# A graph layer on one core: attention denominators inverted in eight rows, and two scalings moved from VectorE to ScalarE

## The chip, the core and the metric

The kernel runs on one core of a Trainium2 chip. A core has TensorE (PE, matmuls), VectorE (DVE), ScalarE (ACT), GpSimd (POOL, which here writes the descriptors of indirect DMAs), SyncE (SP, which here issues plain DMAs), and 16 DMA engines. The metric is the device time of one execution in microseconds (us).

## What is computed

One layer over 6250 nodes of 512 features and 100000 edges sorted by target: a layer norm, a graph convolution (mean of the neighbours' rows, two products, a layer norm), linear attention in 8 heads of 64, and then a mixture of experts on the layer-normed sum. Cut to what matters:

```
xn  = layernorm(x)
q, k, v = heads(xn @ w_qkv.T);  q = elu(q / 8) + 1;  k = elu(k) + 1
denom = (q . sum_n k) per node and head + 1e-8
att = heads_joined(q @ (k^T v) / denom) @ w_out.T + b_out
mean = segment_sum(xn[src], dst) / max(deg, 1)
h   = layernorm(xn @ W_self.T + mean @ W_neigh.T + bias) * gamma + beta
x2  = x + h + att
out = x2 + shared_experts(tn) + top2_of_8_experts(tn),   tn = layernorm(x2)
```

## The kernel before

The nodes are 50 tiles of 125, taken in 25 groups of two (NG, G). There are four stages, each engine with its own written-out program and semaphores between them. First (0 to some 370 us) every row is normalised, split into two float16 halves and written to `table`; keys are made, and their sums and the context are accumulated. The weights are converted beside it. Second (to some 1750 us) comes the loop over the groups that this change touches. Third, the tokens of each expert are gathered, multiplied and written to `yd`. Fourth, the shared experts are computed and all is added up.

In the second stage the work of group i and parts of its neighbours (prev = i-1, nxt = i+1) are interleaved by hand; the order on each engine is the order in which the code is written.

- POOL (L582 to L632): for tile 0 and tile 1 of a group 17 indirect gathers of 128 rows each from `table` into a ring buffer (`gathers`, L591 and L598; ring 0 lies in the space called Wff, ring 1 in region), then four indirect scatters of token numbers into `slots` (`dispatch`, L609) for the group three before the gathered one.
- SP: edge lists (`ebuf`, L389), the transposed rows of the next group (L402), x (L408), and stores of x2 (L413) and of the normalised rows (L418, L420).
- PE (`group`, L1116): query projection (L1125), transposes of the mean (L1136), the products of tile 0 (L304 to L306), `turn_normalised` of prev (L1094), the attention denominators (L1159), `aggregate(nxt, 0)` (L1066 to L1083: 34 products of one-hot matrices with the gathered rows), gate of prev, the products of tile 1, the attention products, `places` of prev, and `aggregate(nxt, 1)`.
- DVE (`group`, L1735): minimum part of the queries (L1742), low halves, query features (L1750), the one-hot matrices of the next tile 0 (`onehots`, L1606 to L1620), the reciprocals (L1758) and products (L1761) of the attention, `means(nxt, 0)` (L1626 to L1632: degree, its reciprocal, and the division of the aggregated rows), gate of prev (L1689 to L1712), the one-hot matrices of the next tile 1, residual and first normalisation (L1774 to L1785), x2 (L1791), the second normalisation (L1380 to L1397, L1797), `means(nxt, 1)`, and `places` of prev (L1718 to L1732). `places` waits, ahead of L1727, until the scatters of `dispatch(i-2)` have landed.
- ACT: Relu and Exp of the queries, high halves (L832, L800, L845), copies out of the turned rows (L808), the denominators plus 1e-8 (L840), and the gate's Exp (L815).

The denominators: `blk_k` is a block-diagonal 128x128 matrix per 128 features with the key sums, so a product gives each of the 128 feature rows its head's denominator; ACT adds 1e-8 on the way out of PSUM, and DVE inverts all 128 rows of 500 elements twice a group.

## Time and profile before

| | |
|---|---|
| median of 3 runs | 2438.61 us (2436.04 to 2452.51) |
| profiled execution, its own time | 2446.38 us |
| its span in the trace | 2444.8 us |
| PE busy | 2094.9 us, 86% |
| DVE busy | 1728.4 us, 71% |
| POOL busy | 1476.3 us, 60% |
| ACT busy | 696.3 us, 28% |
| DMA | 497.58 MB, 204 GB/s over the span |

Busy time does not hold the time in which an engine only issues or waits. The loop of the second stage runs from about 415 us to about 1740 us of the span; its turns take a little over 50 us each. The rows below are read from that stretch: a row of a timeline is one instruction or some equal ones in a row (start, duration, engine, line, operation, output <- inputs, count, and in brackets the idle time before it and what ended it).

### The profile page before, as it was taken

To read this page: it belongs to the slowest core of one execution; us is meant where nothing else is said; L and a number is where in the kernel's file an instruction comes from. 1 tells how busy PE (TensorE), PEld (TensorE's weight loads), DVE (VectorE), ACT (ScalarE), POOL (GpSimd) and SP (SyncE) were. 2 spreads that over 40 slices of the span, in tenths; PEclk is the share of its full clock that TensorE was granted. 3 is DMA by queue.
4 is the path that set the end of the run, shared out by engine and by line. 5 is a ranking of instruction groups with operands and counts; after the bars stand their busy time and mean duration, and the time that the engine had idled before them with its cause. 6 is when DMAs were issued, how large, how long until landed. Compare 5 with 4: busy or idle time off the path is not lost.

```text
span 2444.8 us, 43895 instructions
## 1 busy us (share of the span) xinstructions
PE 2094.9 (86%) x12977; PEld 1395.4 (57%) x12978; DVE 1728.4 (71%) x3445; ACT 696.3 (28%) x1167; POOL 1476.3 (60%) x1470
## 2 busy tenths in 40 slices
PE   5988986898888788888788887888399999879999
PEld 2444543565655455555456555555266666557776
DVE  6888984888888687888688887787444444336666
ACT  3555760211122111112121111221134344323332
POOL 3665666777777777777777777774222223234442
PEclk8999998999989899999899999899599999989999
DMA  9646646777777777777877778876344454456776
GB/s 290 193 133 228 212 139 182 231 240 214 192 237 232 218 217 214 201 211 233 221 222 216 218 193 213 243 225 194 95 153 162 159 168 158 143 189 242 250 249 211
DMA packets 185852, 497.58 MB, mean 204 GB/s; under 512 B 45244, under 2 KB 58044, under 8 KB 183880
## 3 DMA queue, kind: packets, MB, share of 16 engines
q0 software_dynamic: 95984, 309.84, 44.6%
q1 hardware_dynamic: 66649, 135.52, 17.7%
q10 hardware_dynamic: 23167, 51.60, 5.4%
q8 instruction: 24, 0.39, 0.1%
q14 instruction: 28, 0.23, 0.0%
HBM read 373.97 MB, written 122.76 MB: 203 GB/s over the span
## 4 chain that ended last, share of the span: by engine, by line
PE 31%; DVE 30%; issue 14%; POOL 9%; DMA 8%; ACT 5%; DVEq 2%; SPq 1%; POOLq 0%; PEld 0%; ACTq 0%; PEldq 0%
PE bank L304 6%; DVE region L1758 6%; PE bank L305 5%; PE bank L306 5%; DMA region<-table,idx 3%; DMA slots<-tok,posi 3%; PE bank L1214 2%; DVE ohs L1606 2%; POOL Wff L598 2%; POOL region L591 2%; POOL region L540 2%; PE bank L1267 2%; PE bank L1269 2%; PE bank L1268 2%; DVE region L1405 2%
## 5 line engine op out<-in xcount | busy, mean ns | idle before, releaser
L647 POOL DMA_INDIRECT region<-table,idx x122 | 116.2, 952 | 301.0 <-PE bank L1214 264.6
L591 POOL DMA_INDIRECT region<-table,ebuf x225 | 229.1, 1018 | 79.3 <-issue 79.0
L598 POOL DMA_INDIRECT Wff<-table,ebuf x200 | 230.3, 1152 | 61.0 <-issue 61.0
L591 POOL DMA_INDIRECT Wff<-table,ebuf x225 | 221.3, 983 | 69.6 <-issue 69.6
L598 POOL DMA_INDIRECT region<-table,ebuf x200 | 223.9, 1120 | 61.0 <-issue 60.1
L304 PE MATMUL bank<-Wff,region 128*125 128x512 f16 (+1 forms) x636 | 244.8, 385 | 12.4 <-DVE region L1894 7.4
L305 PE MATMUL bank<-Wff,region 128*125 128x512 f16 (+1 forms) x636 | 244.7, 385 | 0.0
L306 PE MATMUL bank<-Wff,region 128*125 128x512 f16 (+1 forms) x636 | 244.1, 384 | 0.0
L304 PE MATMUL bank<-Wsn,region 128*125 128x512 f16 x400 | 176.0, 440 | 70.2 <-ACT region L825 67.8
L825 ACT ACTIVATE region<-bank,sv 128x500 f32<-128x500 f32 x50 | 33.7, 673 | 675.0 <-DVE region L1742 648.1
L1076 PE MATMUL bank<-region,ohs 128*125 128x512 f16 x850 | 195.7, 388 | 26.1 <-DMA region<-table,ebuf 26.1
L1758 DVE RECIPROCAL region<-region 128x500 f32<-128x500 f32 x50 | 163.7, 3273 | 41.7 <-ACT region L840 41.7
L1076 PE MATMUL bank<-Wff 128*125 128x512 f16 x850 | 189.3, 380 | 2.2 <-DMA Wff<-table,ebuf 2.2
L609 POOL DMA_INDIRECT slots<-tok,posi x100 | 129.6, 1296 | 80.4 <-DVE before L1732 50.3
L305 PE MATMUL bank<-Wsn,region 128*125 128x512 f16 x400 | 172.6, 431 | 0.0
L306 PE MATMUL bank<-Wsn,region 128*125 128x512 f16 x400 | 170.5, 426 | 0.0
L1076 PEld LDWEIGHTS bank<-region,ohs 128*125 128x125 f16 x850 | 115.6, 139 | 95.6 <-DMA region<-table,ebuf 31.0
L1859 DVE COPY region<-bank 128x1024 f16<-128x1024 f16 x60 | 41.5, 691 | 174.6 <-PE bank L1214 174.6
L1076 PEld LDWEIGHTS bank<-Wff 128*125 128x125 f16 x850 | 113.5, 137 | 67.3 <-DMA Wff<-table,ebuf 5.0
L1866 DVE SCALAR_TENSOR_TENSOR region<-bank,sv,region 128x512 f32<-128x512 f32 x118 | 88.6, 751 | 73.3 <-PE bank L306 71.2
L1225 PE MATMUL bank<-region,Wff 128*128 128x256 f16 x472 | 129.8, 275 | 1.9 <-DVE region L1859 1.9
L1226 PE MATMUL bank<-region,Wff 128*128 128x256 f16 x472 | 129.8, 275 | 0.0
(298 smaller groups left out, 5432.2 us busy)
## 6 DMA issues: line engine op xcount, KB each, us to landing
yd<-region ACTq DMA_DIRECT2D x59, 512.0 KB, 3.0
x2d<-region SPq DMA_DIRECT2D x25, 512.0 KB, 10.4
table<-region SPq DMA_DIRECT2D x25, 512.0 KB, 4.5
region<-x2d SPq DMA_DIRECT2D x25, 512.0 KB, 5.1
table<-region POOLq DMA_DIRECT2D x50, 250.0 KB, 3.4
xnt<-region POOLq DMA_DIRECT2D x25, 500.0 KB, 4.0
region<-xnt SPq DMA_DIRECT2D x25, 500.0 KB, 5.1
x2t<-region SPq DMA_DIRECT2D x25, 500.0 KB, 4.2
```

What stands on the lines that cost most here:

```text
L304: wmm(ps, xh, wh, start=first, stop=False)
L305: wmm(ps, xh, wl, start=False, stop=False)
L306: return wmm(ps, xl, wh, start=False, stop=last)
L591: pool.indirect_dma_start(out=ring[j][:, s, :], out_offset=None, in_=table, in_offset=bass.IndirectOffsetOnAxis(ap=ebuf[j][:, 2 * s:2 * s ...
L598: pool.indirect_dma_start(out=ring[j][:, s, :], out_offset=None, in_=table, in_offset=bass.IndirectOffsetOnAxis(ap=ebuf[j][:, 2 * s:2 * s ...
L609: pool.indirect_dma_start(out=slots, out_offset=bass.IndirectOffsetOnAxis(ap=posi[:, j, k:k + 1].bitcast(U32), axis=0), in_=tok[:, j:j + 1 ...
L647: pool.indirect_dma_start(out=tg[:, c, :], out_offset=None, in_=table2, in_offset=bass.IndirectOffsetOnAxis(ap=idx[:, 2 * turn + c:2 * tur ...
L1076: last = wmm(bank[6][0:T, :], oh[j][:, s, :], ring[j][:, s, part * D:(part + 1) * D], start=False, stop=False, skip_group_check=True)
L1225: wmm(ps, w1(e, 0, k, c), tTc[:, 0, k, :], start=(k == 0), stop=False)
L1226: wmm(ps, w1(e, 0, k, c), tTc[:, 1, k, :], start=False, stop=False)
L1758: dve.reciprocal(qr[:, cc, :], qr[:, cc, :]).then_inc(sem["q_rec"], 1)
L1866: stt(ysb[:, j, :], bank[4 + j][:, :], sv[:, S_W2:S_W2 + 1], b2bc[:, e, :], ALU.mult, ALU.add).then_inc(sem["y_sb"], 1)
```

## The change

Denominators: `blk_k` is replaced by `key_heads`, [128, 8] per 128 features. Four products, accumulated in one PSUM bank, give 8 rows (one per head) of 250 nodes. DVE adds 1e-8 and inverts these 8 rows in place (`den`). Then PE spreads them to the 128 feature rows of each block by four products with `head_rows` (zeros and ones, 8 x 128), behind `aggregate(nxt, 0)`; the attention product on DVE reads the spread reciprocals from PSUM. ACT's L840 is gone. In DVE's order the attention product now comes behind `means(nxt, 0)`, the gate ahead of the low halves of the queries, and the addition of beta to x ahead of `means(nxt, 0)`. ACT divides the aggregated rows by the degrees, and makes the second normalisation as x2 * rs + nm, with nm = -mean * rs from one small DVE operation. At the start some small matrices of zeros and ones are made.

```diff
-        blk_k = over[:, (OVER - 1) * FFB:(OVER - 1) * FFB + 2 * KC * 128].bitcast(F32).rearrange("p (k n) -> p k n", k=KC)
+        key_heads = tail[:, 0:KC * 8].rearrange("p (k h) -> p k h", k=KC)
+        head_rows = tail[0:8, KC * 8:KC * 8 + KC * 128]
+        den = tail[0:8, KC * 8 + KC * 128:KC * 8 + KC * 128 + GT]
...
+            def means(g, j):
+                divided = of(act, 4 * g + 2 * j + 2)
+                act.wait_ge(sem["consts"], 1)
+                act.wait_ge(sem["deg_step"], divided)
+                if past(g):
+                    act.wait_ge(sem["mt_ps"], 2 * g)
+                act.activation(mean[:, j, :], bank[6][0:T, :], ACT.Copy, scale=dg[:, j, 1:2]).then_inc(sem["mean_sb"], 1)
...
+            def normalised(i):
+                for j in range(G):
+                    act.wait_ge(sem["z_step"], (NORM_STEPS + 1) * (i + 1))
+                    if past(i):
+                        act.wait_ge(sem["tn_lo"], 2 * i)
+                    act.activation(tn[:, j, :], x2[:, j, :], ACT.Identity, scale=rs[:, j, :], bias=nm[:, j, :]).then_inc(sem["tn_sb"], 1)
...
-                for c in range(2):
-                    act.wait_ge(sem["den_ps"], 2 * i + c + 1)
-                    act.activation(qr[:, 2 * c:2 * c + 2, :], two(c), ACT.Identity, bias=tiny[:]).then_inc(sem["q_den"], 1)
+                if nxt is not None:
+                    means(nxt, 0)
...
+                if nxt is not None:
+                    means(nxt, 1)
+                normalised(i)
...
-                        for c in range(2):
-                            pe.wait_ge(sem["q_phi"], 2 * i + c + 1)
-                            for k in range(2):
-                                last = wmm(two(c)[:, k, :], blk_k[:, 2 * c + k, :], qe[:, 2 * c + k, :], start=True, stop=True)
-                            last.then_inc(sem["den_ps"], 1)
+                        for k in range(KC):
+                            pe.wait_ge(sem["q_phi"], 2 * i + k // 2 + 1)
+                            last = wmm(bank[1][0:8, 0:GT], key_heads[:, k, :], qe[:, k, :], start=(k == 0), stop=(k == KC - 1))
+                        last.then_inc(sem["den_ps"], 1)
                         if nxt is not None:
                             aggregate(nxt, 0)
+                        pe.wait_ge(sem["q_rec"], 2 * i + 2)
+                        for c in range(2):
+                            for k in range(2):
+                                last = wmm(two(c)[:, k, :], head_rows[:, (2 * c + k) * 128:(2 * c + k + 1) * 128], den, start=True, stop=True)
+                            last.then_inc(sem["spread_ps"], 1)
...
-                ts(mean[:, j, :], bank[6][0:T, :], dg[:, j, 1:2], None, ALU.mult).then_inc(sem["mean_sb"], 1)
...
             for k in range(KC):
-                ts(blk_k[:, k, :], blk[:], ksum[:, k:k + 1], None, ALU.mult).then_inc(sem["q_u"], 1)
+                ts(key_heads[:, k, :], heads[:, k, :], ksum[:, k:k + 1], None, ALU.mult).then_inc(sem["q_u"], 1)
...
+                dve.wait_ge(sem["den_ps"], i + 1)
+                if past(i):
+                    dve.wait_ge(sem["spread_ps"], 2 * i)
+                ts(den, bank[1][0:8, 0:GT], 1e-8, None, ALU.add).then_inc(sem["q_rec"], 1)
...
+                dve.reciprocal(den, den).then_inc(sem["q_rec"], 1)
+                dve.wait_ge(sem["xg_in"], 32 * (i + 1))
+                tt(xg, xg, beta_bc[0:T, None, :].broadcast_to([T, G, D]), ALU.add).then_inc(sem["h_gam"], 1)
+                if nxt is not None:
+                    means(nxt, 0)
                 for c in range(2):
-                    cc = slice(2 * c, 2 * c + 2)
-                    dve.wait_ge(sem["q_den"], 2 * i + c + 1)
-                    dve.reciprocal(qr[:, cc, :], qr[:, cc, :]).then_inc(sem["q_rec"], 1)
-                    dve.wait_ge(sem["q_rec"], 2 * i + c + 1)
-                    for k in (2 * c, 2 * c + 1):
-                        stt(qe[:, k, :], qe[:, k, :], ksum[:, k:k + 1], qr[:, k, :], ALU.mult, ALU.mult).then_inc(sem["q_hat"], 1)
+                    dve.wait_ge(sem["spread_ps"], 2 * i + c + 1)
+                    for k in range(2):
+                        stt(qe[:, 2 * c + k, :], qe[:, 2 * c + k, :], ksum[:, 2 * c + k:2 * c + k + 1], two(c)[:, k, :], ALU.mult, ALU.mult).then_inc(sem["q_hat"], 1)
+                if prev is not None:
+                    gate(prev)
...
-                for j in range(G):
-                    if past(i):
-                        dve.wait_ge(sem["tn_lo"], 2 * i)
-                    ts(tn[:, j, :], x2[:, j, :], mv[:, j, 0:1], rs[:, j, :], ALU.subtract, ALU.mult).then_inc(sem["tn_sb"], 1)
+                normal(i, x2, sem["x2_sb"], sem["z_step"], XS ** -2, 1)
+                dve.wait_ge(sem["z_step"], NORM_STEPS * (i + 1) + i)
+                stt(nm[:], mv[:, :, 0:1], -1.0, rs[:], ALU.mult, ALU.mult).then_inc(sem["z_step"], 1)
```

POOL's and SP's programs keep their order; only one semaphore that SP waits for at the end of the loop has another name.

The order on DVE, in a steady turn of the loop, from the end of the one-hot matrices of tile 0 to the gate. Before (Wff is the ring's space, `dg` the degrees, `gl` the gate's scores):

```order
L1620 TENSOR_SCALAR iota_f<-iota_f 128x125
L1758 RECIPROCAL region<-region 128x500 [waits q_den]
L1761 SCALAR_TENSOR_TENSOR region<-region,ksum 128x250 [waits q_rec]
L1761 SCALAR_TENSOR_TENSOR region<-region,ksum 128x250
L1758 RECIPROCAL region<-region 128x500 [waits q_den]
L1761 SCALAR_TENSOR_TENSOR region<-region,ksum 128x250 [waits q_rec]
L1761 SCALAR_TENSOR_TENSOR region<-region,ksum 128x250
L1765 TENSOR_TENSOR region<-region 128x500 [waits q_hi] x2
L1625 REGISTER_ALU
L1626 TENSOR_SCALAR dg<-bank 125x1 [waits agg_end]
```

And now (here Wff holds the eight rows `den`, in a part of the same space):

```order
L1657 TENSOR_SCALAR iota_f<-iota_f 128x125
L1794 TENSOR_SCALAR Wff<-bank 8x250 [waits spread_ps,den_ps]
L1798 RECIPROCAL Wff<-Wff 8x250 [waits q_rec,consts]
L1799 REGISTER_ALU
L1800 TENSOR_TENSOR region<-region,beta_bc 125x1024 [waits xg_in]
L1662 REGISTER_ALU
L1663 TENSOR_SCALAR dg<-bank 125x1 [waits agg_end]
L1664 REGISTER_ALU
L1665 RECIPROCAL dg<-dg 125x1 [waits deg_step]
L1806 SCALAR_TENSOR_TENSOR region<-region,ksum,bank 128x250 [waits spread_ps]
L1806 SCALAR_TENSOR_TENSOR region<-region,ksum,bank 128x250
```

The wait for the end of the aggregation (agg_end) now stands ahead of the attention products; it stood behind them.

On ACT, the end of one steady turn and the start of the next (L801 is the division by the degrees, L813 the second normalisation, L846 the Relu of the next group's queries), as it is now:

```order
L865 ACTIVATE region<-region 128x500 [waits att_ps,q_hat]
L832 ISA
L834 ISA [waits gate_dve]
L836 ACTIVATE ge,gs<-gl,gs 125x8 [waits gate_dve]
L837 ACTIVATE ew<-g,gs 125x2
L836 ACTIVATE ge,gs<-gl,gs 125x8
L837 ACTIVATE ew<-g,gs 125x2
L319 REGISTER_ALU
L801 ACTIVATE region<-bank,dg 125x512 [waits mt_ps,deg_step,consts]
L810 REGISTER_ALU
L813 ACTIVATE region<-region,nm,rs 125x512 [waits tn_lo,z_step] x2
```

The work of the last two ACTIVATE lines was DVE's before (L1632 and L1797); on ACT the next group's Relu followed the gate's Exp directly.

## Rows read from the trace of the kernel before

**Rows 1.** Page, part 4: the chain that ended last, by line

```profile
PE bank L304 6%; DVE region L1758 6%; PE bank L305 5%; PE bank L306 5%; DMA region<-table,idx 3%; DMA slots<-tok,posi 3%; PE bank L1214 2%; DVE ohs L1606 2%; POOL Wff L598 2%; POOL region L591 2%; POOL region L540 2%; PE bank L1267 2%; PE bank L1269 2%; PE bank L1268 2%; DVE region L1405 2%
```

**Rows 2.** Busy us (instructions) per stretch: PE, PEld, DVE, ACT, POOL; clock, DMA share, GB/s

```profile
414.90:1667.00 1252.10, 1078.08 (x6103) 719.53 (x6104) 997.31 (x2281) 231.64 (x470) 974.46 (x900) 0.93 0.78 220
561.60:1620.70 1059.10, 906.06 (x5143) 604.59 (x5142) 846.54 (x1963) 196.13 (x400) 823.85 (x761) 0.93 0.78 218
```

**Rows 3.** POOL's timeline: gathers (start us, duration us), idle before in brackets

```profile
389.57 0.95 POOL L591 DMA_INDIRECT region<-table,ebuf  x1 [7.56 <-issue]
...
956.21 0.95 POOL L591 DMA_INDIRECT region<-table,ebuf  x1 [2.95 <-issue]
...
1004.70 2.86 POOL L598 DMA_INDIRECT Wff<-table,ebuf  x1 [0.31 <-issue]
...
1065.67 0.95 POOL L591 DMA_INDIRECT region<-table,ebuf  x1 [0.30 <-issue]
```

**Rows 4.** DVE's timeline: one turn of the loop, from L1742 to L1742

```profile
1048.98 1.38 DVE L1742 TENSOR_SCALAR region<-bank,sv 128x500 f32<-128x500 f32 x2 [0.42 <-issue]
...
1065.79 0.87 DVE L1761 SCALAR_TENSOR_TENSOR region<-region,ksum 128x250 f32<-128x250 f32 x2
...
1073.08 0.23 DVE L1689 SCALAR_TENSOR_TENSOR gl<-bank,sv,gateb_bc 125x16 f32<-125x16 f32 x1
...
1077.59 2.38 DVE L1606 TENSOR_TENSOR ohs<-iota_f,ebuf 128x2125 f16<-128x2125 f32 x1 [1.71 <-issue]
...
1083.53 1.39 DVE L1777 SCALAR_TENSOR_TENSOR region<-bank,sv,bias_bc 125x512 f32<-125x512 f32 x2
...
1096.56 1.00 DVE L1797 TENSOR_SCALAR region<-region,mv,rs 125x512 f32<-125x512 f32 x2
...
1100.47 1.38 DVE L1742 TENSOR_SCALAR region<-bank,sv 128x500 f32<-128x500 f32 x2 [0.43 <-issue]
```

**Rows 5.** DVE's timeline: the wait of `places` for the scatters, once in seven turns

```profile
1211.56 0.17 DVE L1727 CAST posi<-posf 125x4 int32<-125x4 f32 x1 [10.15 <-DMA slots<-tok,posi]
```

**Rows 6.** PE's timeline in the same turn: denominators, then the aggregation of tile 0

```profile
1060.61 1.96 PE L1159 MATMUL bank<-region,Wff 128*128 128x250 f32 x8 [1.55 <-ACT region L808]
...
1063.32 7.53 PE L1076 MATMUL bank<-Wff 128*125 128x512 f16 x34
```

**Rows 7.** DVE, 561.6 to 1620.7 (20 turns): busy us, mean ns | idle before

```profile
L1758 DVE RECIPROCAL region<-region 128x500 f32<-128x500 f32 x40 | 130.9, 3274 | 30.8 <-ACT region L840 30.8
...
L1606 DVE TENSOR_TENSOR ohs<-iota_f,ebuf 128x2125 f16<-128x2125 f32 x20 | 47.5, 2375 | 33.6 <-issue 33.6
L1606 DVE TENSOR_TENSOR Wff<-iota_f,ebuf 128x2125 f16<-128x2125 f32 x20 | 47.5, 2375 | 4.5 <-issue 4.5
...
L1761 DVE SCALAR_TENSOR_TENSOR region<-region,ksum 128x250 f32<-128x250 f32 x80 | 34.8, 477 | 1.4
L1632 DVE TENSOR_SCALAR region<-bank,dg 125x512 f32<-125x512 f32 x40 | 30.0, 751 | 1.8 <-DVE dg L1628 0.5
...
L1765 DVE TENSOR_TENSOR region<-region 128x500 f16<-128x500 f32 x40 | 27.1, 677 | 1.9
...
L1774 DVE TENSOR_TENSOR region<-region,beta_bc 125x1024 f32<-125x1024 f32 x20 | 24.5, 1227 | 0.0
L1797 DVE TENSOR_SCALAR region<-region,mv,rs 125x512 f32<-125x512 f32 x40 | 20.8, 562 | 0.7
...
L1628 DVE RECIPROCAL dg<-dg 125x1 f32<-125x1 f32 x40 | 6.6, 164 | 1.8 <-DVE dg L1626 0.5
```

**Rows 8.** Page, part 5: an ACT operation out of PSUM

```profile
L825 ACT ACTIVATE region<-bank,sv 128x500 f32<-128x500 f32 x50 | 33.7, 673 | 675.0 <-DVE region L1742 648.1
```

**Rows 9.** DVE's timeline in the last group, which has no gathers behind it

```profile
1697.18 3.28 DVE L1758 RECIPROCAL region<-region 128x500 f32<-128x500 f32 x1 [6.97 <-ACT region L840]
...
1710.48 1.40 DVE L1777 SCALAR_TENSOR_TENSOR region<-bank,sv,bias_bc 125x512 f32<-125x512 f32 x2
```

**Rows 10.** POOL's timeline: the first scatter after the last group's places of prev

```profile
1726.17 1.64 POOL L609 DMA_INDIRECT slots<-tok,posi  x1 [31.10 <-DVE before L1732]
```

More of the change, by code:

```diff
@@ L816, in gate, with group @@
                     act.activation(ew[:, j, :], g8[:, j, 0:2], ACT.Exp, bias=gs[:, j, 0:1]).then_inc(sem["gate_exp"], 1)
-            def group(i, prev):
+            def group(i, prev, nxt):
                 for c in range(2):
@@ L1181, in _ @@
             pe.wait_ge(sem["ksum_sb"], 1)
-            pe.wait_ge(sem["q_u"], KC)
+            for k in range(KC):
+                last = pe.transpose(bank[1][0:8, k * 128:(k + 1) * 128], heads[:, k, :], ident[:, :])
+            last.then_inc(sem["heads_ps"], 1)
             aggregate(0, 0)
+            pe.wait_ge(sem["q_u"], 3 * KC + 2)
             turn_largest("mf_max", 1, 1, MH, 1)
```

60 lines of the change are left out of this document (34 added, 26 removed).

## The prediction

> **What bounds the kernel now.** I began with the page's chain that ended last, because it seems to speak for the change: DVE's L1758, the reciprocals of the denominators, holds 6% of the span by itself [rows 1], some 147 us, and the change makes them small. But a chain is followed back from the last instruction through whichever wait ended last, and where two loops run at nearly one pace it may pass through either. So I asked next which engine never waits in the loop.
>
> That is POOL. From the first gather of the loop's steady part to the last it executes 900 instructions in 1252.10 us and is busy for 974.46 us [rows 2]; what is left, 277.6 us, is 0.308 us per instruction. The gap between two gathers that wait for nothing is 0.30 us [rows 3]. At 0.30 us the gaps come to 270 us, so in all of the loop POOL has waited for others for at most 8 us, and one wait alone, ahead of the gather at 956.21, is 2.7 us of it [rows 3]. The larger wait, 7.56 us at 389.57, lies ahead of the loop's steady part and hangs on the context's products. A POOL that does not wait sets the pace. Its pace is 20 turns in 1059.10 us, with 761 = 20 x 38 + 1 instructions (34 gathers and 4 scatters a turn) [rows 2]: 52.96 us a turn.
>
> The other engines' turn is shorter when nothing holds them: DVE's goes from 1048.98 to 1100.47, 51.49 us [rows 4]. They catch up with POOL by 1.5 us a turn, until once in some seven turns DVE stands 10.15 us in `places` for scatters to land [rows 5]. Then they are behind again. That saw tooth costs POOL nearly nothing, and its mean is POOL's turn. In short: from 415 to 1667 us of the span the kernel is bound by POOL's writing of descriptors, and only in the last group, when there is nothing left to gather, is the chain through DVE and PE the bound.
>
> **The change part by part.** POOL's program is unchanged: the same 34 gathers and 4 scatters. So the first term is what the loop's turn becomes if POOL did not exist; it matters only if it rises above 52.96 us.
>
> Ahead of A, the end of the aggregation of tile 0, nothing gets longer. PE makes four products of 250 columns for the denominators as before, 1.96 us [rows 6], and starts the aggregation behind them; it ends with 1063.32 + 7.53 = 1070.85 [rows 6], so A is about 21.9 us after DVE's L1742. What DVE does meanwhile is hidden: the addition on eight rows, the reciprocal, and the addition of beta, 1.23 us [rows 7]. A reciprocal of 8 rows of 250 is not in this trace. Its time goes by the length of a row: 3.27 us for 500 and 0.16 us for 1 [rows 7] give 0.16 + 249 x 6.23 ns = 1.7 us (bounds: 0.16 and 3.27). Even at 3.27 us, begun after the denominators at 1062.6, it and the two additions end by 1068, ahead of A.
>
> After A things stand in a row that stood side by side. The four spreading products have the same number of columns as L1159, so 1.96 us; bounds are 0 (they overlap) and 3.9 us (at half the clock). DVE's four attention products follow each half: 4 x 0.477 = 1.9 us [rows 7], reading one input from PSUM, as L1777 does at no higher price (0.70 us for 512 elements, two overlapping rows in 1.39 us [rows 4]). The second pair ends at about A + 3.0. The gate's scores come 1.96 us later from PE than before, when DVE started on them at A + 2.2 (1073.08 [rows 4]); so at A + 4.1 at the latest. The gate itself lasts until 1077.59 - 1.71 = 1075.88, 2.8 us [rows 4], then the low halves, 2 x 0.68 us [rows 7]: A + 8.3. Before the one-hot matrices of tile 1 DVE idled 33.6 / 20 = 1.7 us a turn, before those of tile 0 4.5 / 20 = 0.2 us [rows 7]; the latter follow plain work that covers the loading of registers, as the low halves now do. So they start between A + 8.5 and A + 10.0, where they started at A + 6.7 before: 1.8 to 3.3 us later. Behind them DVE saves the addition of beta, 1.2 us, the normalisation's 1.00 us [rows 4] less about 0.2 us for the new small operation, and the division by the degrees, 0.75 us [rows 7]: 2.75 us. The division and the normalisation are now ACT's, each about the 0.67 us of a row of 500 out of PSUM [rows 8]: bounds 0.56 us (DVE's own L1797) and 0.75 us (L1632) [rows 7]. ACT makes the division first, no later than DVE did, and has finished the normalisation 1.3 us later, while DVE is in `places` and L1742; its Relu is not late. If that cover is gone, the Relu and all behind it on PE wait up to 1.3 us. The other divisions (tile 0) stand on ACT ahead of the high halves, which need the attention products made after A anyway.
>
> Turn without POOL: 51.49 + (1.8 to 3.3) - 2.75 = 50.5 to 52.0 us. DVE's busy time falls by about 2 x 3.27 + 2 x 0.75 + 1.00 - 2.3 = 6.7 us a turn, but its wait for the aggregation takes most of it. Both ends are below 52.96. The loop keeps POOL's turn, and the saving in it is 0, at most the 8 us that POOL waited.
>
> The second term is the last group, where no aggregation stands between. DVE went from its first reciprocal at 1697.18 to L1777 at 1710.48, 13.3 us [rows 9]. Now, from the same start: addition to the eight rows, 0.4, reciprocal 1.7, spread 2.0, the last pair of attention products 0.9, then the gate. Its scores wait for PE until the spread and the gate's own products are through (A + 2.2 above, so 2.0 + 1.5 after the reciprocal, with 2.8 us of gate behind them), then low halves 1.4: 0.4 + 1.7 + 3.5 + 2.8 + 1.4 = 9.8 us; the addition of beta lies under the spread. L1777 starts 3.5 us earlier, of which I keep 3, since it will also wait for PE's second tile. `places` of prev then starts another 0.8 us earlier (0.2 in place of the 1.00 us of L1797), and POOL's scatters at 1726.17, on which the expert stage hangs, wait for it [rows 10]. Together 3.8 us; bounds 0 and 4.3.
>
> The third is the phase in which the other engines leave the loop: up to 1.5 us earlier than now, or up to the 10 us of a fresh wait [rows 5] later. I take +1. Ahead of the loop small matrices of zeros and ones are made and a 128-wide product becomes 8-wide: tenths of a us, taken as 0.
>
> Sum: 2446.4 of the profiled execution - 3.8 + 1 = 2443.6. That execution is 7.8 us above the median of the runs, 2438.6; the same 2.8 us off the median give 2435.8 us.
>
> **A rule weighed.** Would less work on DVE make POOL itself faster? The gather at 1004.70 took 2.86 instead of 0.95 us [rows 3], so gathers are stretched in places. The gather at 1065.67 took 0.95 us [rows 3], though DVE's attention products, with two inputs in SBUF, ran from 1065.79 to 1066.66 [rows 4]. So what the change takes off DVE did not hold gathers up, and the stretches stay: 0 us. The Trainium skill, SBUF — State Buffer, section Who interferes with whom, says that a VectorE instruction with two SBUF inputs keeps a GpSimd instruction that reads SBUF waiting for its whole duration, and that tensor_scalar can take the shared ports too. By that rule the attention products, now with one input in PSUM, and the normalisation would give POOL time back in every turn.
>
> **The rivals.**
> 1. *The chain is right and DVE bounds.* Then a turn would fall by the 51.49 less 50.5 worked out above or, if the aggregation is no obstacle, by DVE's 6.7 us: 23 turns give 23 to 154 us, 2285 to 2416. Against it stands a POOL without waits. 2%.
> 2. *POOL is freed.* 4 x 0.477 + 2 x 0.56 = 3.0 us a turn [rows 7], 23 turns, 70 us: 2366. This is what the rule above would do here; the trace speaks against it. 3%.
> 3. *Slower: the new row of waits passes POOL's turn.* From A on, aggregation, spread, attention products, gate and one-hot matrices depend on each other, across PE, DVE and ACT. It decides from a turn of 52.96 us, 1.0 us above my upper end: at half clock for the spread (+2) and ACT's Relu late (+1.3) it is 55.3, 2.3 us over POOL: 23 x 2.3 = 53 us, 2489; at 54 us a turn 24 us, 2460. 7%.
> 4. *Same, by more waits for scatters.* If the others catch up by 2.5 us a turn, they meet the 10 us of [rows 5] every four or five turns. POOL pays at most 2.7 us each [rows 3], and the loop may be left 8 us late: 2441 to 2453. 14%.
> 5. *The change does nothing even in the last group,* because scatters landing hold it: 2439. 4%.
>
> **How the numbers follow.** The forecast, 2435.8, has the remaining 70%, within 2428 to 2444. With 4 and 5 and the near part of 3, the range is 2422 to 2458. I call 1% what a measurement can tell from no change: faster by more than that (under 2414) are rivals 1 and 2, 5%; slower (over 2463) is 3, 7%; within it 88%.
>
> **What would show it.** In the profile after: POOL's gathers still 0.30 us apart and 20 turns in 1055 to 1063 us (if 1040 or less, the first term is wrong). DVE's busy time some 150 us lower, with a new idle time ahead of the degrees, waiting for PE, of 4 us or more a turn. A reciprocal of 1.7 us. The spread 1.96 us, with no late Relu on ACT. The last group's L1777 3 us nearer to the denominators. I would be wrong if PE were found to wait for DVE's one-hot matrices or the inverted rows in every turn while POOL waits for a free ring.

## The result, and the profile after

| | before | after |
|---|---|---|
| median of 4 runs | 2440.35 us (2436.04 to 2452.51) | 2484.83 us (2482.95 to 2492.41) |
| ratio, 95% interval | | 1.0177 (1.0144 to 1.0211) |
| span of the profiled execution | 2444.8 us | 2485.1 us |
| DVE busy | 1728.4 us | 1563.8 us |
| POOL busy | 1476.3 us | 1510.0 us |
| ACT busy | 696.3 us | 731.8 us |

The kernel takes 2484.83 us, 44 us more than before; 2435.8 us (range 2422 to 2458) was forecast. Of the runs below, e5 to e8 took 2866 to 2973 us at a time when the kernel before itself took 2835 us, and one execution of e13 took 5156.39 us: of those four only the traces are read, and that execution is in no ratio. DVE does 165 us less work, and the reciprocals have left the chain that ended last, where they held 6% [rows 1]:

```profile
DMA region<-table,idx 4%; PE bank L309 3%; PE bank L310 3%; PE bank L311 3%; PE bank L1246 2%; PE bank L1299 2%; PE bank L1301 2%; PE bank L1300 2%; PE bank L1257 1%; PE bank L1259 1%; PE bank L1258 1%; DMA slots<-tok,posi 1%; DMA idx<-slots 1%; POOL slots L614 0%; POOL Wff L603 0%
```

So the reciprocals are off the chain, and the time did not fall. The second view says where the time went. These are the same stretches as [rows 2], from the third tile's first gather to the last gather, and 20 turns (columns: stretch, length, busy us and instructions of PE, PEld, DVE, ACT, POOL, then clock, DMA share, GB/s):

```profile
415.59:1704.01 1288.42, 1133.17 (x6294) 745.97 (x6294) 843.09 (x2218) 264.67 (x516) 1010.55 (x900) 0.93 0.76 213
567.80:1656.45 1088.65, 951.54 (x5283) 626.39 (x5283) 711.36 (x1895) 224.81 (x440) 853.14 (x761) 0.92 0.76 212
```

The loop takes 1288.4 instead of 1252.1 us, 54.43 instead of 52.96 us a turn. POOL executes the same 900 instructions, and what is left beside its busy time is the same, 277.9 us against 277.6: it waits for the others no more than before. Its own instructions have become longer, 1010.6 against 974.5 us. These 36.1 us are nearly all of the 40.3 us between the two spans; the loop starts 0.7 us later, and the time behind the last gather is 781.1 instead of 777.8 us.

Which instructions became longer is seen in POOL's timeline, of one turn (start us, us, engine, line, operation, in brackets the idle time before):

```profile
1071.64 0.95 POOL L603 DMA_INDIRECT Wff<-table,ebuf  x1 [0.30 <-issue]
1072.89 2.85 POOL L603 DMA_INDIRECT Wff<-table,ebuf  x1 [0.30 <-issue]
1076.05 0.95 POOL L603 DMA_INDIRECT Wff<-table,ebuf  x1 [0.30 <-issue]
1077.31 0.95 POOL L603 DMA_INDIRECT Wff<-table,ebuf  x1 [0.30 <-issue]
1078.56 2.88 POOL L603 DMA_INDIRECT Wff<-table,ebuf  x1 [0.30 <-issue]
1081.74 0.95 POOL L603 DMA_INDIRECT Wff<-table,ebuf  x1 [0.30 <-issue]
```

and DVE's beside it:

```profile
1072.55 2.38 DVE L1643 TENSOR_TENSOR Wff<-iota_f,ebuf 128x2125 f16<-128x2125 f32 x1 [0.19 <-issue]
1074.96 0.68 DVE L1647 TENSOR_TENSOR Wff<-Wff 128x1000 f16<-128x1000 f16 x1
1075.75 1.15 DVE L1652 TENSOR_TENSOR Wff<-Wff 128x500 f16<-128x500 f16 x3
...
1077.34 0.40 DVE L1794 TENSOR_SCALAR Wff<-bank 8x250 f32<-8x250 f32 x1
1077.84 1.70 DVE L1798 RECIPROCAL Wff<-Wff 8x250 f32<-8x250 f32 x1
1079.47 1.15 DVE L1800 TENSOR_TENSOR region<-region,beta_bc 125x1024 f32<-125x1024 f32 x1
1090.59 0.16 DVE L1663 TENSOR_SCALAR dg<-bank 125x1 f32<-125x1 f32 x1 [9.97 <-PE bank L1108]
```

Two gathers take 2.9 instead of 0.95 us. Each ends 0.81 or 0.82 us after the end of a DVE instruction: 1075.74 after L1643 (1074.93), and 1081.44 after L1800 (1080.62). The same holds for all of them. I took every gather over 1.0 us and every scatter over 1.25 us of the loop, with the scatters behind its last gather (undisturbed 0.95 and 1.19), subtracted 0.82 us (1.06 for a scatter) from its end, and looked for the DVE instruction that ended there: in both kernels each of them meets one within 0.05 us. Summed by that DVE line (stretch in us, count):

| DVE instruction at whose end POOL goes on | before | after |
|---|---|---|
| one-hot matrices, L1606 / L1643 | 70.5 (47) | 71.6 (48) |
| addition of beta, L1774 / **L1800** | 3.8 (5) | **45.4 (24)** |
| low halves, L1765 / L1812 | 6.5 (21) | 3.5 (13) |
| split of the normalised rows, L1683 / L1719 | 6.2 (12) | 3.1 (6) |
| first normalisation, L1780 and L1785 / L1823 and L1828 | 5.9 (29) | 10.0 (29) |
| query features, L1750 / L1786 | 4.1 (21) | 3.7 (16) |
| attention products, L1761 / L1806 | 2.1 (11) | 0 |
| second normalisation, L1797 / none | 0.3 (1) | |

So POOL is *held*: a gather that starts while such a DVE instruction runs does its work only when that has ended. The first row is nearly the same in both kernels; the addition of beta now holds a gather once a turn, for 1.9 us, where before it did so five times in all. And it holds POOL before it runs: the gather at 1078.56 starts 0.91 us ahead of L1800, beside the reciprocal of eight rows; others that start up to 1.40 us ahead of L1800 are held as well.

In the turn before the change the gather at 1065.67 [rows 3] passed the attention products L1761 at 1065.79 [rows 4] because it had started 0.12 us ahead of them. The gather at 1004.70 [rows 3] had started inside this instruction:

```profile
1004.36 2.37 DVE L1606 TENSOR_TENSOR Wff<-iota_f,ebuf 128x2125 f16<-128x2125 f32 x1 [0.20 <-issue]
```

### The profile page after: what moved, and what is told of

Read it like the earlier page. It is cut to its first block and busy times, and to the rows that moved or that the text cites. A ratio compares the mean times of both kernels' runs of the same rounds, so it can differ in the third digit from the quotient of the medians.

```text
span 2485.1 us, 44729 instructions
## 1 busy us (share of the span) xinstructions
PE 2153.2 (87%) x13181; PEld 1423.7 (57%) x13182; DVE 1563.8 (63%) x3380; ACT 731.8 (29%) x1217; POOL 1510.0 (61%) x1470
## 5 line engine op out<-in xcount | busy, mean ns | idle before, releaser
L596 POOL DMA_INDIRECT region<-table,ebuf x225 | 252.6, 1123 | 80.8 <-issue 80.8
L801 ACT ACTIVATE region<-bank,dg 125x512 f32<-125x512 f32 x50 | 34.4, 687 | 860.2 <-issue 504.5
L603 POOL DMA_INDIRECT Wff<-table,ebuf x200 | 240.8, 1204 | 60.9 <-issue 60.9
L603 POOL DMA_INDIRECT region<-table,ebuf x200 | 228.9, 1145 | 60.9 <-issue 60.9
L596 POOL DMA_INDIRECT Wff<-table,ebuf x225 | 220.3, 979 | 69.5 <-issue 69.2
L1101 PE MATMUL bank<-Wff 128*125 128x512 f16 x850 | 203.6, 399 | 35.5 <-DMA Wff<-table,ebuf 35.4
L1101 PEld LDWEIGHTS bank<-Wff 128*125 128x125 f16 x850 | 119.2, 144 | 109.0 <-DMA Wff<-table,ebuf 40.5
L1257 PE MATMUL bank<-region,Wff 128*128 128x256 f16 x472 | 129.6, 275 | 2.0 <-ACT region L890 1.0
L1258 PE MATMUL bank<-region,Wff 128*128 128x256 f16 x472 | 129.7, 275 | 0.0
L1259 PE MATMUL bank<-region,Wff 128*128 128x256 f16 x472 | 129.6, 275 | 0.0
```

Of the source, the lines that this page charges most:

```text
L596: pool.indirect_dma_start(out=ring[j][:, s, :], out_offset=None, in_=table, in_offset=bass.IndirectOffsetOnAxis(ap=ebuf[j][:, 2 * s:2 * s ...
L603: pool.indirect_dma_start(out=ring[j][:, s, :], out_offset=None, in_=table, in_offset=bass.IndirectOffsetOnAxis(ap=ebuf[j][:, 2 * s:2 * s ...
L1101: last = wmm(bank[6][0:T, :], oh[j][:, s, :], ring[j][:, s, part * D:(part + 1) * D], start=False, stop=False, skip_group_check=True)
L1257: wmm(ps, w1(e, 0, k, c), tTc[:, 0, k, :], start=(k == 0), stop=False)
L1258: wmm(ps, w1(e, 0, k, c), tTc[:, 1, k, :], start=False, stop=False)
L1259: last = wmm(ps, w1(e, 1, k, c), tTc[:, 0, k, :], start=False, stop=(k == KC - 1))
```

## The experiments

The theory (A): a DVE instruction with two SBUF inputs keeps POOL's next indirect DMA waiting until it ends, and the new place of the addition of beta is what costs. The rivals: (B) the new eight-row reciprocal, which lies in the ring's memory, holds POOL; (C) the new row of waits from PE over DVE and ACT sets the turn. "Turn" and "busy" below are POOL's as above, "held at the addition" is the sum of the stretches that end with the addition of beta in the loop. Ratios are to the kernel before on the same chip. Turn, busy and held are of the profiled run.

| run | median us | ratio (95%) | turn us | POOL busy us | held at the addition us (count) |
|---|---|---|---|---|---|
| before | 2440.35 | | 52.96 | 974.5 | 3.8 (5) |
| after | 2484.83 | 1.0177 (1.0144 to 1.0211) | 54.43 | 1010.5 | 45.4 (24) |
| e1 addition back | 2434.52 | 0.9949 (0.9929 to 0.9969) | 52.52 | 964.9 | 1.4 (2) |
| e2 addition ahead | 2444.54 | 1.0003 (0.9987 to 1.0019) | 52.72 | 969.3 | 0 |
| e3 addition waits | 2459.87 | 1.0057 (1.0037 to 1.0077) | 53.40 | 986.4 | 19.4 (23) |
| e4 before, behind 128 rows | 2455.82 | 1.0040 (1.0023 to 1.0056) | 53.27 | 980.7 | 13.2 (18) |
| e9 128 rows of 250 | 2463.03 | 1.0062 (1.0040 to 1.0084) | 53.72 | 987.2 | 15.9 (24) |
| e12 ACT moves only | 2445.85 | 0.9997 (0.9979 to 1.0015) | 52.94 | 971.2 | 3.2 (4) |
| e5b wait before reciprocal | 2488.84 | 1.0147 (1.0103 to 1.0190) | 54.72 | 1013.8 | 47.5 (24) |
| e13 after, 128 rows | 2455.55 | 1.0046 (1.0030 to 1.0062) | 53.26 | 982.9 | 15.0 (24) |
| e14 after, 32 rows | 2455.27 | 1.0048 (1.0029 to 1.0067) | 53.23 | 984.5 | 4.7 (24), and 10.5 (23) ahead |
| e10 slot by slot | 2408.33 | 0.9841 (0.9805 to 0.9877) | 51.41 | 912.4 | 12.3 (20) |
| e15 slots and ahead | 2390.37 | 0.9784 (0.9761 to 0.9807) | 50.85 | 914.6 | 8.9 (22) |

In all but the last two, POOL's waits for others in the loop are between 0 and 8 us: the turn follows POOL's busy time.

### e1: the addition back at its old place

```diff
-                dve.wait_ge(sem["xg_in"], 32 * (i + 1))
-                tt(xg, xg, beta_bc...)                # ahead of means(nxt, 0)
...
                 if nxt is not None:
                     onehots(nxt, 1)
+                dve.wait_ge(sem["xg_in"], 32 * (i + 1))
+                tt(xg, xg, beta_bc...)
```

> The changed kernel with one edit: the addition of beta to xg (L1800) stands again where it stood before the change, behind the one-hot matrices of tile 1. Theory A (a DVE instruction that reads two operands from SBUF keeps POOL's next indirect DMA from starting its descriptors until it ends, and holds it off already from the moment it is handed to DVE, while the eight-row reciprocal ahead of it still runs): the 24 gathers that end 1.97 us after the start of L1800 become 0.95 us again, their 45 us go, POOL's turn is 52.9 to 53.1 us instead of 54.43, and the time is 2440 to 2452 us. Rival B (the reciprocal on eight rows itself holds POOL, it lies in the ring's part of SBUF): the 24 stretches stay at about 1.6 us each, 2475 to 2486. Rival C (the new row of waits PE, DVE, ACT sets the turn): POOL's stretches may go but it then waits for free rings instead, 2470 to 2486.

Measured: 2434.52 us, 50 us less than the changed kernel, and half a per cent faster than the kernel before. The turn is 52.52 us, even below what was expected:

```profile
415.81:1658.61 1242.80, 1127.98 (x6300) 740.85 (x6301) 840.41 (x2214) 264.12 (x516) 964.92 (x900) 0.94 0.76 221
```

The reciprocal on eight rows is still there and the row of waits too, so rivals B and C fall as causes of the loss: this one moved instruction is all of it. B falls by the trace as well. In e1 24 gathers start inside the eight-row reciprocal, most of them 0.7 us into it as in the changed kernel, and each takes 0.95 us (DVE, then POOL):

```profile
1059.46 1.70 DVE L1798 RECIPROCAL Wff<-Wff 8x250 f32<-8x250 f32 x1
```

```profile
1060.18 0.95 POOL L603 DMA_INDIRECT Wff<-table,ebuf  x1 [0.30 <-issue]
```
Against the kernel before, POOL is busy 9.6 us less in its 900 instructions, since gathers happen to be held a little less at the other DVE instructions too.

### e2: the addition one place earlier

The two lines go between `onehots(nxt, 0)` and the wait for the denominators.

> The changed kernel with the addition of beta one place earlier: behind the one-hot matrices of tile 0 and ahead of the two instructions on the eight rows, so that the instruction ahead of it lasts only 0.23 us. Theory A: it holds POOL for its own 1.15 us alone, and the gather that starts 0.03 us ahead of it passes, as in the kernel before: stretches at this line 0 to 5 us in all, 2438 to 2452. Rival B (the reciprocal holds POOL): 24 gathers are still stretched, now until the reciprocal's end, by 0.5 to 1 us more or less, 2470 to 2486. Rival C: 2475 to 2486.

Measured: 2444.54 us, no stretch at this line in 25 turns. The same instruction costs 45 us behind the reciprocal and nothing two places earlier. That it costs nothing at all is owed to where the gathers fall: 24 of them start 0.02 to 0.04 us ahead of it and pass, while in e3 and e13, where they start inside it, it costs 0.6 to 0.8 us a turn.

### e3: one wait more

```diff
                 dve.wait_ge(sem["xg_in"], 32 * (i + 1))
+                dve.wait_ge(sem["q_rec"], 2 * i + 2)
                 tt(xg, xg, beta_bc...)
```

> The changed kernel with one wait more and nothing moved: DVE waits for the reciprocal's own semaphore before it takes up the addition of beta, so the addition is handed over only when the reciprocal has ended. DVE loses about 0.1 us a turn. Theory A: the gather that starts 0.91 us ahead of the addition passes, the next starts 0.34 us into it and waits for its end, 0.8 us instead of 1.93: 24 x 1.1 = 27 us less stretch, POOL's turn 53.3 to 53.6, 2453 to 2463. A rival in which the addition holds POOL only while it runs and the reciprocal does too (B): no change, 2480 to 2488. Rival C: no change or slower, 2484 to 2490.

Measured: 2459.87 us, as expected: a wait more on the engine makes the kernel 25 us faster. POOL, then DVE, in one turn:

```profile
1125.88 0.95 POOL L596 DMA_INDIRECT region<-table,ebuf  x1 [0.30 <-issue]
1127.13 1.87 POOL L596 DMA_INDIRECT region<-table,ebuf  x1 [0.30 <-issue]
```

```profile
1125.15 1.70 DVE L1798 RECIPROCAL Wff<-Wff 8x250 f32<-8x250 f32 x1
1126.96 1.22 DVE L1801 TENSOR_TENSOR region<-region,beta_bc 125x1024 f32<-125x1024 f32 x1
```

The gather at 1125.88 starts 0.7 us into the reciprocal and passes; in the changed kernel one at the same place was held. So, as in e1, the reciprocal alone does not hold POOL. It is held only with the addition directly behind, until the addition's end, and with a wait between the two it is not held ahead of the addition. In the changed kernel a gather that starts 0.15 us into the reciprocal still passes, and one that starts 0.23 us into it is held. That the addition waits in DVE behind the reciprocal and holds from there is the likely reading; no run shows it.

### e4, e6 and e9: the addition behind reciprocals of 128 rows, in the kernel before

e4 puts it behind the first L1758 with the wait for xg ahead of the reciprocal; e6 the same with the wait between the two; e9 as e4, but the reciprocal is split in two halves of 250 elements.

> The kernel before, with one edit: the addition of beta is moved to right behind the first reciprocal of the denominators (L1758, 128 rows of 500, 3.27 us), with no wait between the two. Theory A: the addition holds POOL from the start of the reciprocal on, 3.3 + 1.2 us, so one gather a turn is stretched by 2.5 to 3.7 us: 60 to 85 us more on POOL, 2490 to 2525. Theory A without the early hold (only while the addition runs): at most 0.9 us a turn, 2440 to 2460. Rival B (something of the eight rows): nothing of them is here, 2436 to 2444. Rival C: the addition only moved, 2436 to 2446.

> The kernel before with the addition of beta behind the first 128-row reciprocal (3.27 us) as in the 4th run, but with its own wait for xg between the two, as the changed kernel has it. Theory A1 (a two-input instruction with a condition of its own holds POOL while it waits behind the running one): POOL is held from the reciprocal's start on, one gather a turn stretched by 2.5 to 3.7 us, 2490 to 2525. Theory A2 (only the eight-row reciprocal does that): as the 4th run, 13 us of stretches at the addition, 2446 to 2462.

> The kernel before with the addition of beta behind a reciprocal of 128 rows of 250 elements (the first reciprocal of 500 is split in two halves, the addition directly behind the second half, DVE's wait for xg ahead of both). So far POOL was held early, from 0.2 us after the reciprocal's start, behind 8 rows of 250, and only from the addition's start behind 128 rows of 500. Theory R (the eight rows do it): no early hold here, no gather that starts more than 0.1 us ahead of the addition is held; stretches at the addition up to 15 us in all, 2444 to 2462. Theory N (the length of 250 elements does it): gathers that start up to 1.4 us ahead of the addition are held too, some 1.5 to 1.9 us each turn, 30 to 45 us in all, 2465 to 2485.

e4 was expected at 2490 to 2525 us and took 2455.82: here the addition holds only gathers that start at most 0.03 us ahead of it. e9 (2463.03) shows the same with 250 elements: POOL, then DVE,

```profile
1077.31 0.95 POOL L591 DMA_INDIRECT region<-table,ebuf  x1 [0.30 <-issue]
1078.56 1.83 POOL L591 DMA_INDIRECT region<-table,ebuf  x1 [0.30 <-issue]
```

```profile
1076.84 1.66 DVE L1761 RECIPROCAL region<-region 128x250 f32<-128x250 f32 x1
1078.41 1.16 DVE L1762 TENSOR_TENSOR region<-region,beta_bc 125x1024 f32<-125x1024 f32 x1
```

where the gather at 1077.31 starts 1.10 us ahead of the addition, inside the reciprocal, and passes. So neither the length nor the lack of a wait makes the early hold. In e6, too, the addition holds none that starts more than 0.1 us ahead of it; 14 gathers and scatters are held there, 0.62 us each.

### e5 and e5b: the wait on the other side of the eight-row reciprocal

The wait for xg goes ahead of `dve.reciprocal(den, den)`; nothing else changes.

> The changed kernel, nothing moved: only DVE's wait for xg, which stood between the eight-row reciprocal and the addition of beta, now stands ahead of the reciprocal, so the addition carries no wait of its own. In the changed kernel POOL is held from 0.2 us after the reciprocal's start, 1.4 us ahead of the addition; in the kernel before with the addition behind the 128-row reciprocal and no wait of its own (4th run) it was held only from the addition's start. Theory A1 (what holds early is a two-input instruction that waits in DVE with a condition of its own): the early hold goes, the stretch is at most 1.1 us instead of 1.93, 2450 to 2466 us. Theory A2 (what holds early is the eight-row reciprocal in front of a two-input instruction, whatever the wait): 24 stretches of 1.9 us as in the changed kernel, 2480 to 2488.

> The fifth run's kernel again, unchanged, because its times came from a chip on which the kernel before took 2835 us and POOL waited for gathers to land. From that run's trace, POOL was held from 1.44 us ahead of the addition or more, whichever side of the reciprocal the wait for xg stands: so here 24 stretches of about 1.9 us at the addition and 2478 to 2490 us; 2450 to 2466 would say that the addition's own wait matters after all.

Measured in e5b: 2488.84 us, 24 gathers held, 47.5 us, most of them 1.0 us ahead of the addition and for 2 us, the earliest 1.21 us ahead. A1 falls: whose wait it is makes no difference.

### e13 and e14: more rows, in the changed kernel

```diff
-                dve.reciprocal(den, den)
+                dve.reciprocal(den_more, den_more)    # 128 (e14: 32) rows; rows 8 and up hold ones
```

> The changed kernel with one edit in the loop: the reciprocal of the denominators runs over 128 rows of 250 instead of 8, in place, at the same place in the order (the other 120 rows hold ones; one memset ahead of the loop). The addition of beta stays directly behind it. Theory R (a reciprocal on few rows lets the next instruction hold POOL from its own start): with 128 rows the early hold goes, the gather that starts 0.91 us ahead of the addition passes, the next waits 0.8 us: some 20 us of stretches at the addition instead of 45, as with the added wait of the third run, 2455 to 2466 us. Rival (the place, the tile or the order does it, not the rows): 24 stretches of 1.9 us, 2478 to 2490.

> The same with 32 rows. Theory R in the form that any part of the 128 rows left idle lets POOL be held early: 24 stretches of about 1.9 us, 2478 to 2490. In the form that only a few rows (up to 16 or so) do it: as with 128 rows, 2455 to 2466. The two forms are even for me.

e13, POOL and DVE:

```profile
1011.91 0.95 POOL L604 DMA_INDIRECT Wff<-table,ebuf  x1 [0.30 <-issue]
1013.17 1.63 POOL L597 DMA_INDIRECT region<-table,ebuf  x1 [0.31 <-issue]
```

```profile
1011.19 1.72 DVE L1800 RECIPROCAL Wff<-Wff 128x250 f32<-128x250 f32 x1
1012.83 1.16 DVE L1802 TENSOR_TENSOR region<-region,beta_bc 125x1024 f32<-125x1024 f32 x1
```

e14, POOL and DVE:

```profile
1018.39 1.44 POOL L597 DMA_INDIRECT region<-table,ebuf  x1 [0.30 <-issue]
1020.13 1.14 POOL L597 DMA_INDIRECT region<-table,ebuf  x1 [0.30 <-issue]
```

```profile
1017.67 1.71 DVE L1800 RECIPROCAL Wff<-Wff 32x250 f32<-32x250 f32 x1
1019.30 1.15 DVE L1802 TENSOR_TENSOR region<-region,beta_bc 125x1024 f32<-125x1024 f32 x1
```

With 128 rows the reciprocal takes as long as with 8 (1.72 us), and the gather that starts 0.92 us ahead of the addition passes: 2455.55 us. That is theory R, at the very place. 32 rows give the same time in another way: the same gather is held, but let go at 1019.01 (its end, 1019.83, less 0.82), 0.29 us before the addition starts, and the next is held by the addition itself. The rows decide, at unchanged duration (whether by their number or by which of the 128 they are was not tested: the 8 and the 32 are the first ones); why few rows in front let the next instruction hold POOL so early is not settled. Neither of e14's two forms describes what came: its time is that of the second, its trace has an early hold as the first had it, but a shorter one.

### e8 and e7: which instructions hold

e8 replaces the addition of beta by `ts(xg, xg, 0.5, None, ALU.add)`, one input (beta is left out of this result); e7 compares the one-hot matrices in float16, in e1's kernel.

> The changed kernel with the addition at its new place behind the reciprocal, but of a constant 0.5 instead of beta (beta is left out of this result): the same 1024 elements in and out, one input from SBUF instead of two. Theory A (two SBUF inputs): the 24 stretches go, as in the first experiment, 2434 to 2450 us. A rival in which any DVE instruction of this size handed over behind the reciprocal holds POOL: the stretches stay, 2475 to 2486.

> The first experiment's kernel (changed kernel, addition back at its old place) with the one-hot matrices compared in float16: the 17 numbers of each partition less the tile's first node, as float16 (a new DVE instruction of 17 elements and its wait, 0.3 to 0.4 us), against a float16 row 0 to 124. The instruction of 2125 elements, float32 and two SBUF inputs, at whose end 48 gathers in the loop wait, 74 us in all, then reads float16 as the additions behind it, beside which no gather was stretched. If theory A's hold comes from two float32 inputs: these 74 us go, POOL's turn could fall to 49.8 us, and then the chain of DVE and PE sets it, 51 to 52 us; 23 x 1 to 1.8 us less than the first experiment: 2390 to 2415. If float16 holds POOL as well: the stretches stay, 2430 to 2445. If the comparison is slower in this form and DVE's chain the bound: above 2440.

Both expectations on theory A failed. In e8 15 gathers and scatters are held at the addition, 18.1 us in the loop, those that start up to 1.38 us ahead of it too; POOL, then DVE:

```profile
879.61 2.48 POOL L603 DMA_INDIRECT region<-table,ebuf  x1 [0.30 <-issue]
```

```profile
880.66 0.62 DVE L1800 TENSOR_SCALAR region<-region 125x1024 f32<-125x1024 f32 x1
```

The gather ends 0.81 us after the DVE instruction, though that has one SBUF input. So two inputs are no condition of a hold, late or early. It handles 1024 elements in 0.62 us, where the reciprocals, beside which gathers pass, are slow (1.7 us for 250). The second normalisation of the kernel before, L1797, has one input and 0.56 us for 512 elements: of the gathers that start in it those up to 0.13 us after its start pass, one at 0.14 us is held by 0.26 us, so it stays open whether it holds.

In e7 the 2125-element comparison takes 2.38 us in float16 as it did in float32, and 42 of the 47 in the loop hold a gather, 61.9 us. So float16 is no way out. The expectation had argued that no gather was stretched beside the float16 additions; in the changed kernel that is so only because the gathers always start at the same places beside them, the nearest 0.12 us before the end of one (1076.05, L1652). In e10 below, where they start at other places, the 14 gathers and scatters that start 0.05 to 0.26 us inside the 1000-element addition are held to its end:

```profile
502.15 1.32 POOL L598 DMA_INDIRECT Wff<-table,ebuf  x1 [0.30 <-issue]
```

```profile
501.98 0.68 DVE L1654 TENSOR_TENSOR Wff<-ohs 128x1000 f16<-128x1000 f16 x1
```

(POOL, then DVE. The gather starts 0.17 us into the addition and ends 0.81 us after its end.) So the additions hold as well. A hold of under 0.13 us does not show: an undisturbed gather takes 0.95 us, a held one ends 0.82 us after its holder.

The Trainium skill, SBUF — State Buffer, section Who interferes with whom, says that VectorE with two SBUF inputs, or in its faster modes that use a second port, shares that port with GpSimd, and that the holder keeps the other out for the whole instruction. The held gathers here agree, to 0.05 us, and e8's one-input instruction, 1024 elements in 0.62 us, fits the second case; no run shows in which mode it ran. The section also infers that such a `tensor_tensor` leaves the writing of descriptors alone; 45 and 71 us of stretches say otherwise, and the measurement decides.

### e12: the ScalarE part alone

> The kernel before with the ScalarE part of the change alone: the division by degrees and the second normalisation go to ACT, the denominators stay as they were, the addition of beta stays at its old place. Theory A (POOL's instructions set the loop's pace, and only DVE instructions that hold it matter): the two divisions read PSUM and held nothing, the normalisation held at most 0.3 us in all, so POOL's turn stays 52.8 to 53.1 and the time is 2436 to 2448. Rival (DVE's work counts): 1.7 us a turn less, 39 us, 2400 to 2410. Rival (the ACT part costs): above 2460.

Measured: 2445.85 us, ratio 0.9997; turn 52.94 us. DVE has 45 us less work in 20 turns (801.54 busy against 846.54 [rows 2]), and nothing comes of it:

```profile
557.49:1616.39 1058.90, 894.77 (x5146) 597.93 (x5146) 801.54 (x1903) 251.79 (x480) 823.46 (x761) 0.94 0.79 218
```

### e10 and e15: shorter holds on purpose

If POOL sets the turn and DVE holds it, the 71 us at the one-hot matrices are to be had. e10 is e1 with

```diff
-                    tt(oh[j], iota_f[:, None, :]..., ebuf[j][:, 1:2 * SLOTS:2]..., ALU.is_equal)
+                    ts(rel[j], ebuf[j][:, 1:2 * SLOTS:2], iota_f[:, 0:1], None, ALU.subtract)
+                    for s in range(SLOTS):
+                        ts(oh[j][:, s, :], iota16, rel[j][:, s:s + 1], None, ALU.is_equal)
```

and e15 has the addition of beta at e2's place as well.

> The first experiment's kernel (changed kernel, addition at its old place), with each one-hot matrix made by 17 DVE instructions of 125 float16 elements (a row 0 to 124 compared with one number per partition) instead of one of 2125 elements with two SBUF inputs, behind a small subtraction that brings the 17 numbers to the tile's range. Theory A (a holding instruction keeps POOL's next indirect DMA until it ends, and no longer): each of the 17 can hold it for about 0.15 us at most, so the 74 us of stretches at this line fall to 10 us or less, POOL's turn to 49.5 to 50.5 us; if 17 of them last no longer than 3 us, DVE's and PE's chain then sets the turn at 51 to 52.5 us, POOL waits for free rings, and the time is 2405 to 2440. Rival (POOL is held through all 17, because one holding instruction is taken up right behind another): the stretches stay at 1.5 to 2.5 us per matrix, 2435 to 2460.

> The changed kernel with both edits that took stretches away: the one-hot matrices slot by slot (10th run) and the addition of beta ahead of the two instructions on the eight rows (2nd run) instead of at its old place. The 10th run left 12 us of stretches at the addition and POOL waited 25 us for others, turn 51.4 us. If PE's and DVE's chain sets the turn now: the addition ahead of the denominators is hidden under DVE's wait for the aggregation, up to 1.1 us a turn shorter, 2385 to 2405 us. If POOL still sets it: within 5 us of the 10th run, 2402 to 2412.

e10 takes 2408.33, e15 2390.37 us, 2.2% less than the kernel before and 3.8% less than the changed one. The 17 short instructions last 2.87 us, 0.5 us longer than the one, and POOL's gathers pass beside them (DVE, then POOL, then the 20 turns of e10 and of e15):

```profile
1047.99 2.87 DVE L1651 TENSOR_SCALAR Wff<-iota_i 128x125 f16<-128x125 f16 x17
```

```profile
1047.98 0.95 POOL L605 DMA_INDIRECT Wff<-table,ebuf  x1 [0.30 <-issue]
1049.23 1.01 POOL L605 DMA_INDIRECT Wff<-table,ebuf  x1 [0.30 <-issue]
```

```profile
552.39:1580.57 1028.18, 937.67 (x5354) 620.94 (x5353) 750.15 (x2607) 224.71 (x440) 772.58 (x761) 0.96 0.81 225
553.58:1570.58 1017.00, 939.86 (x5352) 621.93 (x5351) 752.13 (x2608) 225.15 (x440) 775.45 (x761) 0.96 0.80 227
```

POOL's busy time in 20 turns falls from 823.85 to 772.58 us, 2.56 us a turn, but e10's turn only by 1.55: POOL now waits 25 us in the loop (12 in e15). Here at last something other than POOL sets part of the pace. The addition's place ahead of the denominators, under DVE's wait for the aggregation, is then worth 0.56 us a turn, as the first case of e15's expectation has it.

## Why the prediction was wrong

- **POOL bounds the loop, and goes on to do so: right.** POOL waits no more after than before, and e12 shows that DVE's time is worth nothing there.
- **"POOL's program is unchanged", so its turn is, and "the stretches stay: 0 us": the step that failed.** The number of POOL's instructions was unchanged, their length was not. The prediction asked only whether less work on DVE could make POOL faster, and took the answer (nothing) for both directions; it never asked what the moved addition would do. The 1.47 us a turn are this term, put at 0: the stretches at the addition of beta went from 3.8 to 45.4 us, and e1 takes them and the whole loss away.
- **"What the change takes off DVE did not hold gathers up": right in size, by wrong reading.** The stretches that belonged to the removed work were 2.1 us (L1761) and some tenths (L1797), so rival 2's 70 us were not there. But the row it was read from, the gather at 1065.67, proved nothing: it had started ahead of L1761. What counts is whether POOL's instruction starts inside DVE's. The stretched gather at 1004.70, in the same group of rows, was not compared with DVE's row beside it; its end, 0.83 us after L1606's, would have told the rule.
- **DVE's terms: right, or nearly.** The reciprocal of 8 x 250 takes 1.70 us (1.7 worked out), the division on ACT 0.69 and the normalisation 0.80 us (0.67). The new idle time ahead of the degrees is 154.2 us in 22 turns, 7 us each ("4 us or more"), and the one-hot matrices of tile 1 start 8.1 us after A, 0.4 us below the lower bound (8.5 to 10.0). DVE's busy time fell by 165 us (150). The waits of `places` for scatters grew, as rival 4 said, from 29.2 us in 3 waits of the loop to 54.3 us in 11, and cost POOL nothing (DVE's waits in the changed kernel: us in all, times, the longest):

```profile
DVE dg L1663 <- PE bank L1108: 154.2, 22, 12.9
DVE posi L1763 <- DMA slots<-tok,posi: 54.3, 11, 11.2
```

- **The last group, -3.8 us: mis-sized.** DVE, then POOL's first scatters of the last two groups:

```profile
1736.83 0.41 DVE L1794 TENSOR_SCALAR Wff<-bank 8x250 f32<-8x250 f32 x1 [7.25 <-PE bank L1183]
1737.34 1.70 DVE L1798 RECIPROCAL Wff<-Wff 8x250 f32<-8x250 f32 x1
...
1744.49 0.23 DVE L1725 SCALAR_TENSOR_TENSOR gl<-bank,sv,gateb_bc 125x16 f32<-125x16 f32 x1 [1.79 <-PE bank L311]
...
1748.18 0.74 DVE L1818 SCALAR_TENSOR_TENSOR region<-bank,sv,bias_bc 125x512 f32<-125x512 f32 x1
1751.03 0.75 DVE L1818 SCALAR_TENSOR_TENSOR region<-bank,sv,bias_bc 125x512 f32<-125x512 f32 x1 [2.10 <-PE bank L311]
```

```profile
1765.24 1.22 POOL L614 DMA_INDIRECT slots<-tok,posi  x1 [30.81 <-DVE before L1768]
```

The second L1818 ends 14.95 us after the denominators; its like before ended after 14.70 (1710.48 + 1.40 - 1697.18 [rows 9]). DVE's own 9.8 us were 11.4, and then it waits 2.10 us for PE's second tile, which now has the spread ahead of it. From the denominators to the scatters it is 28.4 us, against 29.0 [rows 9, 10]: 0.6 us, all from the shorter normalisation. The text had named this wait and kept 0.5 us for it. Of the 3.5 us, DVE's own row takes 1.6 and this wait the rest.
- **The phase, +1: of the right sign, too small.** From the last gather to the denominators of the last group it is 32.8 us, before 30.1 [rows 2, 9], so +2.7.
- **Rival 3 had the sign and a size (2460 to 2489), for a reason that did not occur.** It wanted POOL to wait for the others, and POOL waits no more than before: that the measured 2484.83 us lies there is luck.

## What to carry to other kernels

Where GpSimd's descriptor writing is the bound, VectorE's work is not free though it is off the path: look, for each indirect DMA, beside which VectorE instruction it starts, and compare its end with that instruction's. A moved instruction is to be priced at its new place against the engine that is held, not only against its own. A bound engine without waits can still be slowed, so its busy time per instruction belongs among the forecasts; and the way to win here was to make the holding instructions shorter and to place them well, not to take work away.

## What was not expected of the hardware

- A DVE instruction that holds POOL holds it also while the instruction ahead of it runs, if that one is a reciprocal on 8 rows and no wait on it stands between (e3): gathers that start up to 1.40 us before the addition were held, behind 128 rows none that starts over 0.1 us before it (e4, e9, e13), in e9 and e13 at the same 1.7 us of duration. With 32 rows there is a hold too, which ends 0.29 us before the addition. The cause is open.
- The turn locks DVE and POOL together: a gather released by the one-hot matrices starts the same row of gathers 1.25 us apart each time, so that the next gather stood 0.91 us ahead of the addition in most turns (in 17 of 24 within 0.03 us). What an instruction costs POOL is then not an average over chances but the same every turn, and a small shift changes it much: in the changed kernel the gather that starts 1.48 us ahead of the addition passes, and the one that starts 1.40 us ahead is held for 2.4 us.
- A comparison of 2125 elements with a repeated operand takes 2.38 us in float32 and in float16 alike; 17 instructions of 125 elements with one number per row take 2.87 us and stretch none of the 183 gathers that start among them in e10 and e15 by more than 0.1 us.
